# Delta-rule stage of a two-layer sequence kernel: three groups of TensorE instructions change places within each chunk step

## Reference, cut to what matters

```python
qkv = conv(x @ W_in)            # causal, 4 taps, per channel; then silu
q = l2norm(q) / 8; k = l2norm(k); beta = sigmoid(b); g = -A * softplus(a + dt_bias)
def step(S, (q, k, v, g, beta)):
    S = S * exp(g)
    S = S + outer(k, (v - k @ S) * beta)
    return S, q @ S
y = rmsnorm(y) * norm_w * silu(z);  x = x + y @ W_o
```

## Time and profile before

| what | value |
|---|---|
| runs of the kernel | 4637.02, 4636.9, 4659.84 us; median 4637.02 us |
| the profiled execution, its own time | 4655.05 us |
| its span, first to last instruction | 4653.3 us |
| mean granted PE clock over the span | 0.897 of 2.4 GHz |
| busy: PE, PEld, DVE, ACT, POOL | 83%, 60%, 67%, 37%, 34% |

### The profile page before, as it was taken

The page is one execution under the profiler, slowest core; times in us unless marked ns, Lnnn a source line. Parts: engine busy times, 40 slices in busy tenths (PEclk is TensorE's granted clock), DMA queues, the critical chain, the costliest instruction groups (busy, mean ns, idle before and its releaser), DMA issues. The chain is left out here.

```text
span 4653.3 us, 163745 instructions
## 1 busy us (share of the span) xinstructions
PE 3861.4 (83%) x66245; PEld 2812.4 (60%) x66245; DVE 3117.4 (67%) x6104; ACT 1733.8 (37%) x3495; POOL 1595.7 (34%) x2519
## 2 busy tenths in 40 slices
PE   6999999866648998989988989989899998588860
PEld 4666666533326776767776767767677766455530
DVE  3777777747746676767666766767677654288858
ACT  1222222224423343444443433434444432277750
POOL 1333333311004454444444444544444443100001
PEclk6998999988858999999999999999999987699975
DMA  0222222136522222222222222222222221111105
GB/s 25 44 47 46 55 56 49 42 84 155 158 65 49 42 56 41 47 51 48 50 47 49 48 49 40 57 42 47 51 48 49 49 47 26 55 27 28 28 18 149
DMA packets 695281, 251.77 MB, mean 54 GB/s; under 512 B 529368, under 2 KB 660128, under 8 KB 694176
## 3 DMA queue, kind: packets, MB, share of 16 engines
q1 hardware_dynamic: 694560, 241.62, 23.7%
HBM read 154.63 MB, written 86.79 MB: 52 GB/s over the span
## 5 line engine op out<-in xcount | busy, mean ns | idle before, releaser
L1373 POOL TENSOR_TENSOR d_f<-d_ms,d_mhalf 128x16 f32<-128x16 f32 x64 | 239.5, 3742 | 965.1 <-DVE d_ms L1807 965.1
L1567 PE MATMUL d_pa<-d_wv,d_hs 128*128 128x512 f32 x1024 | 517.6, 652 | 0.9 <-DVE d_qk L1778 0.4
L1761 DVE SCALAR_TENSOR_TENSOR d_acc<-d_pa,d_cq,d_acc 128x512 f32<-128x512 f32 x576 | 431.7, 750 | 95.2 <-ACT d_acc L1406 80.3
L1383 POOL TENSOR_TENSOR d_prod<-d_ablk,d_tblk 128x15 f32<-128x15 f32 (+7 forms) x960 | 342.5, 357 | 218.5 <-DMA d_ablk<-a_blocks 147.9
L1387 POOL TENSOR_TENSOR d_tblk<-d_tblk,d_prod 128x28 f32<-128x28 f32 (+7 forms) x896 | 336.4, 375 | 70.8 <-POOL d_prod L1383 0.2
L1567 PEld LDWEIGHTS d_pa<-d_wv,d_hs 128*128 128x128 f32 x1024 | 219.5, 215 | 232.1 <-issue 220.2
L1542 PE MATMUL d_pa<-d_hq,d_wqk 128*128 128x259 f32 x768 | 255.4, 462 | 81.4 <-DVE d_acc L1761 58.0
L1406 ACT ACTIVATE d_acc<-d_pa,d_cq 128x512 f32<-128x512 f32 x192 | 131.9, 687 | 420.8 <-PE d_pa L1542 418.0
L262 POOL TENSOR_TENSOR a_act<-a_act,a_cws 128x512 f32<-128x512 f32 x128 | 166.8, 1316 | 310.2 <-DMA a_cws<-cw_rows 165.3
L1580 PEld LDWEIGHTS d_pb<-d_of_head,d_sqT 128*128 128x128 f32 x2048 | 246.2, 196 | 39.2 <-issue 39.0
L1370 POOL TENSOR_TENSOR d_nr<-d_n,d_half_power 128x16 f32<-128x16 f32 x64 | 188.0, 2938 | 193.8 <-DVE d_n L1846 179.8
(11 more groups left out here) (371 smaller groups left out, 9418.3 us busy)
## 6 DMA issues: line engine op xcount, KB each, us to landing
a_cws<-cw_rows SPq DMA_DIRECT2D x32, 1024.0 KB, 10.5
decays<-g_dec SPq DMA_DIRECT2D x16, 2048.0 KB, 7.3
d_dd<-decays SPq DMA_DIRECT2D x64, 512.0 KB, 4.3
d_hs<-h_t SPq DMA_DIRECT2D x512, 32.0 KB, 2.2
t_blocks<-d_tblk SPq DMA_DIRECT2D x128, 128.0 KB, 1.7
a_blocks<-d_at SPq DMA_DIRECT2D x512, 16.0 KB, 1.9
d_ablk<-a_blocks SPq DMA_DIRECT2D x64, 128.0 KB, 2.1
d_tt<-t_blocks SPq DMA_DIRECT2D x512, 16.0 KB
```

The costliest lines, as they stand in the source:

```text
L1373: pool.tensor_tensor(f[:, :], ms[:, :], mhalf[:, :], ALU.pow).then_inc(sem("f_ready"), 1)
L1383: link(pool.tensor_tensor(prod[:, 0:n, 0:s + 1], ablk[:, s, s + 1:SB].unsqueeze(2).to_broadcast([P, n, s + 1]), tblk[:, 0, s, 0:s + 1].uns ...
L1567: last = pe.matmul(pa[:, B + m, :], hs[:, u % 2, t, :], wv[:, t, cols(m)], start=(t == 0), stop=(t == TAPS - 1))
L1761: last = dve.scalar_tensor_tensor(out=own, in0=raw(e)[:, :, t:t + QT], scalar=cq[:, t, col:col + 1], in1=own, op0=ALU.mult, op1=ALU.add)
```

## The change

Only PE's order changes, and one DVE instruction follows it. `conv(0)` stands before the first set. The second set is cut into four loops: `joined(0)`, `joined(1)` (the products of L1638, eight heads each) and `joined_back(0)`, `joined_back(1)` (those of L1634); tap 0 of the second value half stands behind `joined(0)`, tap 1 behind `joined(1)`, taps 2 and 3 behind the whole set, and `conv(2)` behind those. The sums of query squares, with their two waits, stand behind the chunk's output, and DVE's tq behind its two additions into o. No instruction is added or removed, and ACT's, POOL's and SP's programs are as before.

```diff
@@ helpers of PE
-            def project_v(p, u, m):
-                for t in range(TAPS):
+            def project_v(u, m, taps):
+                for t in taps:
                     last = pe.matmul(pa[:, B + m, :], hs[:, u % 2, t, :], wv[:, t, cols(m)],
                                      start=(t == 0), stop=(t == TAPS - 1))
-                last.then_inc(sem("v_sum"), 1)
+                if TAPS - 1 in taps:
+                    last.then_inc(sem("v_sum"), 1)
+            def fourths(u, m):
+                for h in range(HH * m, HH * m + HH):
+                    for b, w in BLOCKS:
...
+            def joined(m):
+                for h in range(HH * m, HH * m + HH):
+                    for b, w in BLOCKS:
+                        rows = rows_of(b, w)
+                        last = pe.matmul(pb[rows, 1, (DH + h) * SB:(DH + h + 1) * SB], w4[rows, h, :],
+                                         tt[rows, h, HB * w + SB:HB * w + HB], start=True, stop=True)
+                return last
+            def joined_back(m):
+                for h in range(HH * m, HH * m + HH):
+                    for b in SEQS:
+                        rows = rows_of(b, 0)
+                        last = pe.matmul(pb[rows, 0, (DH + h) * SB:(DH + h + 1) * SB], tt[rows, h, 0:HB], w4[rows, h, 0:SB],
+                                         start=True, stop=True)
+                return last
@@ PE, iteration
+                if cv:
+                    conv(p, u, 0)
                 if now:
                     hold(sem("ti_loaded"), 16 * 6 * (i + 1))
                     if past:
                         hold(sem("x_used"), i - 1 + X_AHEAD)
...
+                    fourths(u, 0)
+                    fourths(u, 1).then_inc(sem("w4_sum"), 1)
-                if cv:
-                    conv(p, u, 0)
...
-                    project_v(p, u + 1, 0)
+                    project_v(u + 1, 0, range(TAPS))
                 if cv:
                     conv(p, u, 1)
                 if now:
...
+                    joined(0)
+                if then:
+                    project_v(u + 1, 1, (0,))
+                if now:
+                    joined(1)
+                if then:
+                    project_v(u + 1, 1, (1,))
+                if now:
+                    joined_back(0)
+                    joined_back(1).then_inc(sem("t4_sum"), 1)
+                if then:
+                    project_v(u + 1, 1, (2, 3))
                 if cv:
                     conv(p, u, 2)
-                if then:
-                    project_v(p, u + 1, 1)
...
-                if far:
-                    hold(sem("n4_ready"), n + 1)
-                    hold(sem("q_squared"), n + 1)
-                    sum_squares(1).then_inc(sem("q_summed"), 1)
                 if now:
...
                         last.then_inc(sem("o_sum"), 1)
+                if far:
+                    hold(sem("n4_ready"), n + 1)
+                    hold(sem("q_squared"), n + 1)
+                    sum_squares(1).then_inc(sem("q_summed"), 1)
@@ DVE, iteration
-                if far:
-                    dve.wait_ge(sem("q_summed"), n + 1)
-                    dve.tensor_scalar(tq[:, (u + 2) % 4, :], ...).then_inc(sem("tq_ready"), 1)
                 if now:
...
                     last.then_inc(sem("o_ready"), 1)
+                if far:
+                    dve.wait_ge(sem("q_summed"), n + 1)
+                    dve.tensor_scalar(tq[:, (u + 2) % 4, :], ...).then_inc(sem("tq_ready"), 1)
```

More of the change, by code:

```diff
@@ L1563, in against_state @@
                 return last
-            def project_v(p, u, m):
-                for t in range(TAPS):
+            def project_v(u, m, taps):
+                for t in taps:
                     last = pe.matmul(pa[:, B + m, :], hs[:, u % 2, t, :], wv[:, t, cols(m)],
                                      start=(t == 0), stop=(t == TAPS - 1))
-                last.then_inc(sem("v_sum"), 1)
+                if TAPS - 1 in taps:
[4 more added lines that the diff above has]
+                        rows = rows_of(b, w)
+                        last = pe.matmul(pb[rows, 0, h * SB:(h + 1) * SB], at[rows, u % 2, h, HB * w:HB * w + HB],
+                                         ti[rows, h, HB:HB + SB], start=True, stop=True)
+                return last
+            def joined(m):
+                for h in range(HH * m, HH * m + HH):
+                    for b, w in BLOCKS:
+                        rows = rows_of(b, w)
+                        last = pe.matmul(pb[rows, 1, (DH + h) * SB:(DH + h + 1) * SB], w4[rows, h, :],
[7 more added lines that the diff above has]
+                                         start=True, stop=True)
+                return last
             def turn_keys(u):
@@ L1881, in iteration @@
                     dve.tensor_tensor(xo[:, :], xt[:, :], pb[:, 0, 0:D], ALU.add).then_inc(sem("x_used"), 1)
-                if far:
-                    dve.wait_ge(sem("q_summed"), n + 1)
-                    dve.tensor_scalar(tq[:, (u + 2) % 4, :], pb[:, 1, DH:2 * DH], DHD * RMS_EPS,
-                                      DHD * RMS_EPS * L2_EPS, ALU.mult, ALU.add).then_inc(sem("tq_ready"), 1)
                 if now:
@@ L1895, in iteration @@
                     last.then_inc(sem("o_ready"), 1)
+                if far:
+                    dve.wait_ge(sem("q_summed"), n + 1)
+                    dve.tensor_scalar(tq[:, (u + 2) % 4, :], pb[:, 1, DH:2 * DH], DHD * RMS_EPS,
+                                      DHD * RMS_EPS * L2_EPS, ALU.mult, ALU.add).then_inc(sem("tq_ready"), 1)
                 made[part] += links[0]
```

## The result

The changed kernel takes 4860.83 us (median of 4 runs, 4843.11 to 4866.69) against 4636.96 us beside it: ratio 1.0469, 95% interval 1.0422 to 1.0515. It is 4.7% slower; 1.8% was forecast.

A forecast was written before the change was run, and what follows sets the result against it. PE's own work bounds the kernel, with instruction stops and low clock costing about 23 us a pass. Seven passes at +10.9 us give 76, steps outside add 16 and shed 10: +82 us, 4719 us median, range 4615 to 4795.

The forecast's parts named there:

- conv(3)'s wait less that of the fourth set: Ahead of conv(3): 2.2 us idle on DVE, less the fourth set's 0.46 us; net +1.75 us a step.
- conv(0)'s wait on qk, with the gaps around it: Ahead of conv(0), now before the first set: PE idles for DVE's first qk, +0.6 us a step.
- stops of both sets: At L1612 and L1638: PE's stops for instruction blocks fall from 12.1 to some 2 us a pass.
- loop's end and the step behind it: Slow products cover the loop's stop, -1.3 us a pass; the next step's conv(0) waits for nothing, 0.6 us.
- second set cut by taps: In the second set (L1638, L1634): changes between large and small products cost +0.3 us a step.
- query squares, PE's work: Query squares moved behind the chunk's output: PE's work stays the same, 0 us.
- clock: shed some 10, added 11.6: Low clock behind the sets' stops goes; new low clock behind conv(3)'s wait adds +1.45 us a step.
- I take 1.7 us in 85 of 100 steps: Behind conv(3)'s wait: a low clock stretch costs 1.7 us in 85 of 100 steps, +1.45 us a step.
- The first (the clock stays): Rival: conv(3)'s wait comes but the clock stays at 2.4 GHz, 4637 us within some 20; chance 0.17.
- the second rival: At L1612 and L1638 instruction supply alone decides, conv(3) waits under about 0.5 us: 4534 us; chance 0.15.
- The third (the stops stay): Rival: the sets' stops only move by a few products, half of the 20 us stay: 4789 us; chance 0.13.

The follow-up runs named there:

- e3: The old kernel with only conv(2) moved, behind the second value half: 4910.99 us, ratio 1.0583 to the old kernel.
- e2: The changed kernel with conv(2) directly behind the second set, ahead of value taps 2 and 3: 4581.03 us, ratio 0.9895 to the old kernel.
- e13: The changed kernel with conv(2) as the second set's second cut, ACT taking it before its four copies, value taps 1, 2, 3 behind the set: 4566.08 us.
- e14: e13 with the first half of z (two products) between conv(3) and the fourth set: 4656.69 us, ratio 1.0027 to the old kernel.
- e1: The changed kernel with two more value products, their result unused, ahead of conv(3): 4727.69 us, ratio 1.0188 to the old kernel.

## Why the prediction was wrong

The direction and the mechanism held: slower, through conv(3)'s wait and the clock behind it. The size did not, and 4861 us lies above the range. By the prediction's own steps, in us a pass (eight steps):

| step of the prediction | predicted | measured |
|---|---|---|
| conv(3)'s wait less that of the fourth set | +14.0 | +13.0 (100.3 and 22.1 over 6) |
| conv(0)'s wait on qk, with the gaps around it | +4.8 | +2.6 |
| stops of both sets | 12.1 to some 2 | 12.1 to 0.9 |
| loop's end and the step behind it | -1.9 | -1.25 |
| second set cut by taps | +2.4 | +5.5 |
| query squares, PE's work | 0 | +2.7 |
| clock: shed some 10, added 11.6 | +1.6 | +14 to 16 |
| pass | +10.9 | +25.8 |

- **The term that failed is the clock: "I take 1.7 us in 85 of 100 steps".** The share was right (36 of 42), the size was not: where the term had 1.45 us a step, conv(2)'s place cost 3.4 in e3 and 2.9 in the changed kernel. The latter is its difference to e2, which has conv(2) elsewhere and nothing else: 23.2 us of busy time and 54 us of low clock a pass (66.6 and 12.5). I priced the low stretch by the earlier trace rows, where eight value products lie behind the stop and the low level ends after 3.41 us. Behind conv(3) lie the fourth set, z, the sums of squares and the solution; where z did not bring the clock back (8 of 42 steps), it stayed low to the turned keys. The old kernel could have told me: its step of 45.29 us at a mean of 0.89 spent some 10 us at the low level, and I took the shortest stretch. In all the low time grew by 34.7 us a pass, which at 0.45 is 16; what the other lines of the table leave of 25.8 is 14.
- **The wait itself was right**: 2.2 predicted, 2.1 measured, on the link named, and the 0.46 us at the fourth set gone. The steps came out at 39.3 to 47.3 us, not at 39 to 41, through the clock. (In the part on conv(0) the value products should stand at 2181.91, not 2181.95, which changes no term.)
- **The cut set was put too low.** "I take 0.3": from the second set's start to the third set 6.64 us became 7.33 (3274.62 to 3281.95). L1595's 64 products alone take 1.19 us, 18.6 ns each; L1586's 64 take 0.73 us, 11.4 ns. The Trainium skill, "TensorE: Matmul & The Clock Gate", part 3, has a weight load overlap running products only where it goes to another row group; the trace agrees in the price, at products of equal width, though it does not show which loads overlapped. I should have taken that price.
- **The squares were not free.** The old tail, from the output projection to the next keys against keys:

```profile
2206.15 2.05 PE L1717 MATMUL d_pb<-d_wo,d_yT 128*128 128x128 f32 x16
...
2211.62 0.27 PE L1561 MATMUL d_pc<-d_state,d_kq 64*64 64x64 f32 x1
2211.62 0.22 PE L1734 MATMUL d_pa<-d_y,d_qk 64*64 64x64 f32 x1
```

  Here the last outputs and the first keys against the state ran into each other. With the squares between them (3301.32 to 3303.27 above) they don't, and 6.77 us became 7.11.
- **The stops were right in sum and wrong in which part takes them**: conv(0) and the squares each take a part, and only both take all of the first set's.
- **Rivals.** The first (the clock stays) falls with e3 and e2: behind 2.1 us the clock falls, behind 0.87 us it stays. e2 and e13 go the second rival's way, to 4581 and 4566 us where it had 4534. The third (the stops stay) falls with the stops, 0.9 us a pass.

## What to carry to other kernels

Price a wait by two things: its length, and what the engine runs behind it, since a wait of some 2 us brought mostly 3.41 us of low clock ahead of the eight value products and up to 13.65 ahead of conv(3) and the fourth set. When a product that others depend on is moved back, count what is left between it and its consumer. Here two taps between conv(2) and conv(3) decided between 4.7% slower and 1% faster. A part that looks free by its operations can still set how instructions reach the engine, so undo the parts one at a time before giving any of them the credit.

## What the hardware showed that I had not expected

- A wait of 0.87 us in front of conv(3) never lowered the clock (0 of 42 steps, e2), one of 2.1 us did in 36 of 42; yet in e14 0.6 to 0.8 us ahead of the small products of the key sums was followed by a low stretch in 31 of 48 steps. Length alone doesn't decide. What else does was not settled.
- The low level can last through steady work: for the 13.65 us at 0.50 shown above PE was busy throughout by the profile, with small products for most of it.
- What takes the stops away can lie far from where they stand: 16 slow products ahead of the keys against the state (1.95 us) thin out the stops of a set some 130 products later, and with eight instructions more in a step (e1) 5 us of them a pass were back. That PE resumes just after a packet of instructions has landed is shown above; that the phase of a step against these blocks of 256 decides where the stops fall is my reading and was not tried by itself.
